# Keeping the keys and values of the last twelve batches on chip for a second cross attention, and exchanging two copies

## What is computed

```python
q = heads(LN(x) @ Wq.T + bq)        # 16 heads of 16 features
k = heads(ctx @ Wk.T + bk)          # ctx: 64 batches x 257 rows x 256
v = heads(ctx @ Wv.T + bv)
attn = softmax(q @ k.T / 4)         # per batch and head: 32 x 257
x = x + merge(attn @ v) @ Wo.T + bo
```

## Time and profile before

| what | value |
|---|---|
| device time, median of 3 runs | 1705.42 us (1704.83 to 1706.88) |
| the profiled execution | 1704.21 us, of which the span is 1702.4 us |
| busy in the span | PE 91%, PE weight loads 71%, DVE 68%, ACT 48%, POOL 35% |
| DMA | 218.43 MB, mean 128 GB/s |
| mean granted TensorE clock | 0.955 of full speed |

### The profile page before, as it was taken

How to read it: one execution, slowest core, us unless ns; L and a number is a source line. 1 busy time by engine, 2 the same in 40 slices (tenths; PEclk the granted TensorE clock), 3 DMA queues, 4 the chain that set the end, 5 groups by cost and what they waited for, 6 DMA issues and landing times. The chain is left out here.

```text
span 1702.4 us, 39132 instructions
## 1 busy us (share of the span) xinstructions
PE 1550.2 (91%) x15530; PEld 1204.2 (71%) x15530; DVE 1153.1 (68%) x2441; ACT 813.4 (48%) x1815; POOL 594.9 (35%) x501
## 2 busy tenths in 40 slices
PE   6988989999998899999999788888889788999998
PEld 3444467555576589999998555666678688599997
DVE  4576869982057456777762446888689777578887
ACT  1232752121134436666664327777637622566664
POOL 2330200000011047865633325677559653112210
PEclk8897999999989989999999899999989899999999
DMA  9993049621023467676745854766200010001001
GB/s 293 325 318 98 1 145 226 125 54 44 1 93 112 121 197 271 241 242 205 235 152 145 244 184 136 230 201 197 80 25 1 16 29 4 13 13 38 20 7 50
DMA packets 151364, 218.43 MB, mean 128 GB/s; under 512 B 38353, under 2 KB 124753, under 8 KB 145297
## 3 DMA queue, kind: packets, MB, share of 16 engines
q1 hardware_dynamic: 115008, 107.80, 22.6%
q0 software_dynamic: 10368, 58.47, 10.7%
q10 hardware_dynamic: 25808, 49.68, 9.0%
HBM read 168.85 MB, written 47.05 MB: 127 GB/s over the span
## 5 line engine op out<-in xcount | busy, mean ns | idle before, releaser
L321 PE MATMUL ps<-kv_ctx,kv_w 128*128 128x257 f32 x512 | 138.6, 407 | 18.9 <-PEq L1743 8.1
L2209 POOL TENSOR_TENSOR a_pr<-a_pr,a_inv 128x1028 f32<-128x1028 f32 x64 | 121.9, 1906 | 71.8 <-DVE a_inv L2321 71.4
L325 PE MATMUL ps<-kv_w,kv_ctx 128*128 128x256 f32 x512 | 131.6, 403 | 13.7 <-ACT kv_kv L345 13.7
L321 PEld LDWEIGHTS ps<-kv_ctx,kv_w 128*128 128x128 f32 x512 | 97.7, 203 | 41.1 <-issue 16.4
L325 PEld LDWEIGHTS ps<-kv_w,kv_ctx 128*128 128x128 f32 x512 | 99.8, 201 | 37.1 <-ACT kv_kv L345 22.0
L2297 ACT ACTIVATE a_pr<-ps,a_neg 128x257 f32<-128x257 f32 x256 | 117.8, 480 | 0.6 <-DVE a_neg L2340 0.6
L1556 POOL TENSOR_TENSOR b0m_pm<-b_dr,b_gates 128x256 f32<-128x256 f32 x16 | 13.2, 831 | 289.7 <-SPq L1520 260.8
L111 PE MATMUL ps<-f_xTH,f_w1H 128*128 128x256 f32 x368 | 106.7, 290 | 1.5 <-DVE f_xTL L1952 1.5
L2046 DVE TENSOR_TENSOR f_hL<-f_hr,f_hH 128x512 fp32r<-128x512 f32 x92 | 75.6, 847 | 45.3 <-ACT f_hH L1895 45.2
L3190 DVE SCALAR_TENSOR_TENSOR x<-ps,g_gate,x 128x256 f32<-128x256 f32 x256 | 105.2, 475 | 0.0
L112 PE MATMUL ps<-f_xTL,f_w1H 128*128 128x256 f32 x368 | 104.8, 285 | 0.0
(11 more groups left out here) (416 smaller groups left out, 4470.5 us busy)
## 6 DMA issues: line engine op xcount, KB each, us to landing
a_kv<-kv SPq DMA_DIRECT2D x64, 513.0 KB, 4.0
kv<-kv_kv ACTq DMA_DIRECT2D x53, 513.0 KB, 5.7
a_ctxT<-in_ctxT SPq DMA_DIRECT2D x32, 514.0 KB, 8.0
a_ctxR<-in_ctx SPq DMA_DIRECT2D x32, 512.0 KB
kv_ctx<-in_ctxT ACTq DMA_DIRECT2D x61, 257.0 KB, 3.3
outs<-f_yo SPq DMA_DIRECT2D x23, 256.0 KB, 2.6
a_vB<-vlast SPq DMA_DIRECT2D x16, 256.0 KB
kv<-f_kv ACTq DMA_DIRECT2D x5, 513.0 KB, 10.6
```

The source lines that it names most:

```text
L321: done = e.matmul(out[:, 0:NK], self.w[:, 0, c, cols(part)], ctx[:, c, :], start=(c == 0), stop=(c == DC - 1))
L325: done = e.matmul(out[:, cols(t, D)], ctx[:, c, cols(t)], self.w[:, 1, c, :], start=(c == 0), stop=(c == DC - 1))
L2209: e.tensor_tensor(pr[:, b % RP, :, :], pr[:, b % RP, :, :], inv[:, b % 2, :].unsqueeze(2).to_broadcast([P, HG, NK]), ALU.mult).then_inc(*p ...
```

## The change

The last twelve batches (52 to 63) are no longer stored and loaded again. Their keys and values are written straight into a tile of twelve places (KeysKept) where the loop reads them; it lies where the expert layer held its first weights and one half of its hidden values. Batches 52 to 56 are formed there in the expert layer's tail, 57 to 63 in the second cross attention. The loop takes these twelve first: its i-th batch is (i + 52) mod 64, and the later ones are loaded twelve ahead into the same places. The values of the last key are stored in the new order, in two pieces, and loaded four batches at a time. The row tiles of x are finished in the new order. In the loop VectorE now copies the first turn and ScalarE the second, one step later; ScalarE also does the first instruction of the weighted pair; the exponents and the maxima are split in two halves with other work between them. The weighting of a new pair waits for the pair before it, where it waited for the one two before.

```diff
@@ -31,6 +31,7 @@
+KEPT = 12
@@ -263,6 +265,33 @@
+class KeysKept:
...
+    def __init__(self, K):
+        self.Y = Layer(K, "late")
+        self.at = self.Y.sb("kv", [P, KEPT, KV])
...
+    def places(self, first, last):
+        return [KeptPlace(self.at[:, b - (B - KEPT), :]) for b in range(first, last)]
...
+    def close(self):
+        self.Y.close()
...
+class KeptPlace:
...
+    def __init__(self, at):
+        self.at = at
...
+    def free(self, e):
+        pass
...
+    def store(self, e, out):
+        pass
@@ -1666,6 +1695,10 @@
+    with Layer(K, "f0w") as Y:
+        w1 = [Y.sb(f"w1{n}", [P, 2, DC, FC * P], F32R) for n in "HL"]
+        high = Y.sb("hH", [P, 2, FC, BLOCK], F32R)
+    K.late = KeysKept(K)
@@ -1733,8 +1765,9 @@
-        A.host(AHEAD[4], (0, 1, 2, 3), A.own + [kv2, kv3, kv1])
-        assert AHEAD[4] % 5 == 2
+        first, kept = sum(AHEAD[:4]), B - KEPT
+        stored = [(A.own + [kv2, kv3, kv1])[n % 5] for n in range(kept - first)]
+        A.host(AHEAD[4], (0, 1, 2, 3), stored + K.late.places(kept, first + AHEAD[4]))
@@ -2064,7 +2097,7 @@
-    HG, RV, LB, SB, RP, RAMP = 4, 8, 8, 6, 4, 4
+    HG, RV, LB, SB, RP, RAMP = 4, KEPT, 4, 6, 4, 4
@@ -2072,21 +2105,23 @@
-        kv = sb("kv", [P, RV, KV])
+        kv = K.late.at
...
         neg, tot, inv = (sb(n, [P, 2, HG]) for n in ("neg", "tot", "inv"))
...
-        def load(e, b):
-            e.dma_start(kv[:, b % RV, :], K.kv[b]).then_inc(*ld_kv[b % RV].up(16))
+        def batch(i):
+            return (i + B - KEPT) % B
...
+        def load(e, i):
+            e.dma_start(kv[:, i % RV, :], K.kv[batch(i)]).then_inc(*ld_kv[i % RV].up(16))
@@ -2100,7 +2135,7 @@
-            A.host(AHEAD[5], (6, 7), A.own + [kv1])
+            A.host(AHEAD[5], (6, 7), K.late.places(B - AHEAD[5], B))
@@ -2124,11 +2159,10 @@
-                    for b in range(RV):
-                        load(e, b)
...
-                    e.dma_start(K.vlast, vlm[:, :]).then_inc(*d_vl.up(16))
-                    e.wait_ge(*d_vl.at(16))
+                    e.dma_start(K.vlast[0:KEPT, :], vlm[B - KEPT:B, :]).then_inc(*d_vl.up(16))
+                    e.dma_start(K.vlast[KEPT:B, :], vlm[0:B - KEPT, :]).then_inc(*d_vl.up(16))
+                    e.wait_ge(*d_vl.at(32))
                     for j in range(2):
@@ -2172,13 +2206,16 @@
+        rows = [batch(BT * n) // BT for n in range(NT)]
+        K.norms["s"].order = rows
@@ -2208,28 +2245,31 @@
-                    if b >= 2 * LB and b % 2:
-                        K.next.piece(e, (b - 2 * LB) // 2)
+                    if b >= 16 and b % 2:
+                        K.next.piece(e, (b - 16) // 2)
...
                 def scores(b):
-                    e.wait_ge(*ld_kv[b % RV].at(16 * (b // RV + 1)))
+                    if b < KEPT:
+                        e.wait_ge(*A.ev.at(3 * (batch(b) + 1)))
+                    else:
+                        e.wait_ge(*ld_kv[b % RV].at(16 * (b // RV)))
                     if b:
...
-                                            qb[own, c, b, :, :].rearrange("p h q -> p (h q)"), kT(b, c)[own, :], start=True, stop=True)
+                                            qb[own, c, batch(b), :, :].rearrange("p h q -> p (h q)"), kT(b, c)[own, :], start=True, stop=True)
...
                     if t:
-                        e.wait_ge(*a_T.at(b + 1))
+                        e.wait_ge(*v_T.at(b + 1))
                     elif b:
-                        e.wait_ge(*v_T.at(b))
+                        e.wait_ge(*a_T.at(b))
                     for r in range(HG):
@@ -2237,8 +2277,8 @@
-                    if b >= 4:
-                        e.wait_ge(*v_oT.at((b - 4) // 2 + 1))
+                    if b >= 2:
+                        e.wait_ge(*v_oT.at((b - 2) // 2 + 1))
@@ -2285,31 +2325,43 @@
             def _(e):
-                def exponents(b):
-                    if b >= 2:
-                        e.wait_ge(*v_inv.at(b - 1))
-                    if b >= RP:
-                        e.wait_ge(*t_T.at(2 * (b - RP) + 2))
-                        e.wait_ge(*v_last.at(b - RP + 1))
-                    for r in range(HG):
-                        if r % 2 == 0:
-                            e.wait_ge(*v_mx.at(2 * b + r // 2 + 1))
+                def exponents(b, side):
+                    if side == 0:
+                        if b >= 2:
+                            e.wait_ge(*v_inv.at(b - 1))
+                        if b >= RP:
+                            e.wait_ge(*t_T.at(2 * (b - RP) + 2))
+                            e.wait_ge(*v_last.at(b - RP + 1))
+                    e.wait_ge(*v_mx.at(2 * b + side + 1))
+                    for r in (2 * side, 2 * side + 1):
...
                 def turned(b):
-                    e.wait_ge(*t_T.at(2 * b + 1))
+                    e.wait_ge(*t_T.at(2 * b + 2))
                     if b >= 2:
...
-                    e.activation(prT[:, b % 2, 0, :, :], K.ps[:, 6, :].rearrange("p (g n) -> p g n", g=HG), ACT.Copy).then_inc(*a_T.up())
-                for i in range(B + 4):
+                    e.activation(prT[:, b % 2, 1, :, :], K.ps[:, 6, :].rearrange("p (g n) -> p g n", g=HG), ACT.Copy).then_inc(*a_T.up())
...
+                def half_weighed(n):
...
+                    e.wait_ge(*t_P.at(2 * n + 2))
+                    if n:
+                        e.wait_ge(*v_oT.at(n))
+                    out = out_pair(n).rearrange("p c b (h q) -> p c b h q", h=2)
+                    e.activation(half[:, :, :, :], out[:, :, :, 0, :], ACT.Copy, scale=K.parity[:, 0:1]).then_inc(*a_half.up())
...
+                for i in range(B + 5):
                     if has(i - 1):
-                        exponents(i - 1)
+                        exponents(i - 1, 0)
+                    if i % 2 == 0 and has(i - 6):
+                        half_weighed((i - 6) // 2)
+                    if has(i - 4):
+                        turned(i - 4)
+                    if has(i - 1):
+                        exponents(i - 1, 1)
                     if i < 3:
...
-                    if has(i - 3):
-                        turned(i - 3)
@@ -2322,45 +2374,45 @@
-                    e.wait_ge(*t_P.at(2 * n + 2))
-                    if n:
-                        e.wait_ge(*v_oT.at(n))
+                    e.wait_ge(*a_half.at(n + 1))
...
-                    e.tensor_scalar(half[:, :, :, :], out[:, :, :, 0, :], K.parity[:, 0:1], None, ALU.mult).then_inc(*v_half.up())
-                    e.wait_ge(*v_half.at(n + 1))
-                    e.scalar_tensor_tensor(oT[:, :, cols(n, 2 * L)].rearrange("p c (b q) -> p c b q", b=2), out[:, :, :, 1, :],
+                    at = batch(2 * n) // 2
+                    e.scalar_tensor_tensor(oT[:, :, cols(at, 2 * L)].rearrange("p c (b q) -> p c b q", b=2), out[:, :, :, 1, :],
...
-                def maxima(b):
+                def maxima(b, side):
...
-                    for r in (0, 2):
-                        at = bank(b, r)
-                        e.tensor_reduce(neg[:, b % 2, r:r + 2], K.ps[:, at:at + 2, 0:NK], AX.X, ALU.max, negate=True).then_inc(*v_mx.up())
+                    r = 2 * side
+                    at = bank(b, r)
+                    e.tensor_reduce(neg[:, b % 2, r:r + 2], K.ps[:, at:at + 2, 0:NK], AX.X, ALU.max, negate=True).then_inc(*v_mx.up())
...
                 def turned(b):
-                    e.wait_ge(*t_T.at(2 * b + 2))
+                    e.wait_ge(*t_T.at(2 * b + 1))
                     if b >= 2:
...
-                    e.tensor_copy(prT[:, b % 2, 1, :, :], K.ps[:, 6, :].rearrange("p (g n) -> p g n", g=HG)).then_inc(*v_T.up())
+                    e.tensor_copy(prT[:, b % 2, 0, :, :], K.ps[:, 6, :].rearrange("p (g n) -> p g n", g=HG)).then_inc(*v_T.up())
...
-                for i in range(B + 4):
...
+                for i in range(B + 5):
+                    if i % 2 == 0 and has(i - 6):
+                        weighed((i - 6) // 2)
                     if has(i):
-                        maxima(i)
+                        maxima(i, 0)
+                    if has(i - 3):
+                        turned(i - 3)
+                    if has(i):
+                        maxima(i, 1)
                     if has(i - 1):
...
-                    if has(i - 4) and i % 2:
-                        weighed((i - 4) // 2)
-                    if has(i - 3):
-                        turned(i - 3)
                 for t in range(NT):
@@ -2369,20 +2421,21 @@
             def _(e):
-                for b in range(RV, B):
-                    e.wait_ge(*t_P.at(b - RV + 1))
-                    load(e, b)
-                    done = b - RV + 1
+                for done in range(1, B - LB):
+                    e.wait_ge(*t_P.at(done))
+                    if done - 1 + RV < B:
+                        load(e, done - 1 + RV)
...
-                    if done % LB == 0 and 2 <= j < B // LB:
+                    if done % LB == 0 and j < B // LB:
...
-                    if done == LB:
```

(4 more changed lines are left out.)

34 lines of the change are left out of this document (17 added, 17 removed).

## The result

The changed kernel took 1676.65 us (median of 4 runs, 1675.34 to 1688.1), the kernel before 1705.12 on the same chip: a ratio of 0.9848, 95% interval 0.9804 to 0.9893. It is 28.5 us faster by the medians. The forecast was 1689.5 with a range from 1682 to 1698, so the sign was right and the forecast gain of 15.6 us was too small by almost half. Medians and ratios in this document leave out the few executions that ran in a slower state of the chip.

What follows compares the result with a forecast made beforehand. A ring of waits, no engine full, was taken to set the loop's pace, crowded DMA the stretches ahead. Terms 1.8 + 5.4 + 0.3 + 8.1 = 15.6 us off the median 1705.42 gave 1689.8, said as 1689.5; range 1682 to 1698.

Steps and rivals of the forecast that it cites:

- Batch loop and its drain: Second cross attention's batch loop and tail: exchanged copies bring 3.025 us a batch to 2.89, 8.1 us over 60.
- Steps of the ring: Batch loop: two transpose sets sharing a PSUM bank and their copies, steps 0.67, 0.74, 0.66, 0.82, sum 2.89 us.
- the single stumbles: Batch loop: 2.7 us above 57 x 3.025 in the kernel before, left in by the forecast.
- Rival 2: Batch loop goes under the ring's floor, exponents' path decides at 2.75 us a batch: 1681; chance 0.12.
- Query stage: Before the batch loop: dropped stores, loads and buffer waits give back 5.4 us, from 3 to 6.
- Tail: End of the first expert layer: last gather sooner without five stores, and no last store; 1.8 us, 0.3 to 2.9.
- First batches: Start of the batch loop: ScalarE's store just ahead of its exponential table load goes, 0.3 us.
- Rival 4: Kept keys' layout costs something elsewhere, or the transfers' relief is swallowed: within 3 us of before, 1703; chance 0.04.
- Rival 1: Batch loop: the exchange does nothing, another queue takes its place, only the transfers pay: 1698; chance 0.14.
- rival 3: Batch loop: last values, loaded four batches at a time, come late and VectorE waits: slower, up to 1756; chance 0.04.

Runs made afterwards that it cites:

- the first pair: Profiles of the kernel before and the changed kernel shown with the result: 1705.12 and 1676.65 us, ratio 0.9848.
- the lengthened ring: Changed kernel plus a one-column ScalarE copy in each batch, between the wait for the second transposes and their copy: 1690.41 us (0.9860).
- the first experiments' chip: Chip of four kernels against the kernel before: kept keys only 0.9908, exchange only 0.9971, kernel before again 0.9999, changed kernel again 0.9886.
- the exchange alone: Kernel before, all keys stored and loaded, plus swapped copies, split maxima and exponents, and ScalarE's mask: 0.9971 (0.9948 to 0.9993).
- the third pair: Kernel before and changed kernel, both unchanged, run again on a later chip: 1699.49 and 1674.90 us, ratio 0.9842.
- the experiment with stores: Changed kernel, but the twelve kept batches are also stored, 513 KB each, and still not loaded: 1693.89 us, 0.9886.
- the kernel with the places alone: Kernel before with only the SBUF tile places of the change, nothing kept and nothing exchanged: 0.9977 (0.9950 to 1.0003).
- the two halves: Each half of the change alone against the kernel before: kept keys only 0.9908, exchanged copies with split maxima, exponents and ScalarE mask 0.9971.

## Why the prediction was too small

The mechanisms named were all there. The miss is in the size of the tail, and in what had no term: the places of tiles, TensorE's clock ahead of the loop, and the difference between two executions. In the first pair, against which the forecast stands, most of the miss is what had no term: 8.98 + 1.77 of the 28.5 us lie outside the stretches that were priced, and these came to 16.95 against 15.6. That they came so near is luck: there the tail's larger gain was hidden.

- **Batch loop and its drain, forecast 8.1.** Right: 8.51 in the first pair, 8.48 in the third. Steps of the ring, period and equal batches came as written. That the sum fits to 0.4 us is in part luck: the period fell by 0.115 and not 0.135, which is 6.6 us over 57 batches, and the other 1.8 came from the single stumbles, which the forecast left in at 2.7 us and of which 0.9 remained. Rival 2, a ring under its floor, is out: the period is 2.91, not 2.75, and the lengthened ring answers with 0.09.
- **Query stage, forecast 5.4, from 3 to 6.** 4.98 in the first pair; over the profiles 49.0 us in five with the old stores and buffers and 42.4 in the seven of kept keys without added stores or loads, 6.6. But two things are mixed in this. One is the time that TensorE lost in waits, which the forecast priced: TensorE's idle time fell from between 5.4 and 8.5 us to 2.0 in each of the seven. The other is its clock, which had no term: the seven differ among themselves by 2.9 us (40.6 to 43.5) at the same idle time, with granted clocks from 1.00 to 0.93. The cleanest comparison is of two kernels of the first experiments' chip, both at 1.00, the exchange alone and then the changed kernel (window, length, then busy time of TensorE, its weight loads, VectorE, ScalarE and GpSimd; clock, DMA share, GB/s):

```profile
985.43:1030.75 45.32, 39.90 (x161) 26.77 (x161) 19.60 (x34) 13.11 (x33) 10.99 (x16) 1.00 0.81 238
981.69:1022.31 40.62, 38.63 (x160) 26.74 (x161) 19.59 (x34) 13.67 (x33) 10.98 (x16) 1.00 0.26 72
```

  That is 4.7 us, within the range and near the 5.4. The stores by themselves are 1.0 of it (idle time 3.0 against 2.0 us with and without them) and the loads by themselves nothing. By elimination the other 3.7 are ScalarE's waits for buffers, or stores and loads acting together; these two were not separated.
- **Tail, forecast 1.8, from 0.3 to 2.9.** This is the step that failed, and by its reason. It let the last gather start 1.1 us sooner and gave it the lowest landing of the earlier trace rows, 5.7 us. The last gathers did not start sooner. They landed in 2.7, since the stores that shared the 16 DMA engines with them at the end were gone. The lowest landing under load is no floor for a landing without load. The sum also had a slip: a landing counts from the start of the issue (the last gather after starts at 950.40 and its addition 2.74 later), and the forecast added the 5.7 to the end of the issue, 956.9 instead of 956.0, which made the term 0.9 us too small by its own numbers. The page of the Trainium skill that the prediction weighed (DMA: Bandwidth & Descriptors, Anatomy of one DMA) gave an estimated 2.3 us for a gather without traffic, and 3.4 us more in the sum; the trace after agrees with it to 0.4 us. The first pair showed only 2.33 in the tail, inside the range by luck, because its gathers took 2.28 longer to start (46.77 us from first to last, against 44.49), which ate half of the 4.20 us won behind the last one (6.94 against 2.74); the third pair shows the 5.95, and the experiment with stores 7.2.
- **First batches, forecast 0.3.** 1.13 and 3.96 in the two pairs, 25.1 against 23.3 us over the profiles. Here too the length goes with TensorE's clock, 0.74 to 0.93 in the profiles. The two kernels of the third pair stood at 0.74 and 0.92, those of the first pair at 0.80 and 0.79, and at 0.93 and 0.92 the kernel with the places alone took 22.90 and the changed one 22.17. So at the same clock the change gives 0.7 to 1.1 us, and the rest is the clock. The forecast had counted the shorter period from the seventh batch on only; six batches of 0.115 are another 0.7. Whether the change itself raises the clock is not shown.
- **No term: the places of tiles.** 1.8 us in the expert layer ahead of the tail over all profiles, 2.3 in the first pair. Rival 4 had thought of a cost of the layout; it was a gain.

Together 1.8 (places) + 5.9 (tail, by the third pair) + 6.6 (query stage) + 1.8 (first batches) + 8.5 (loop) = 24.6 us, of which 2 to 3 are the clock's. It lies between the 19.5 us of the chip whose tail hides its share and the 26.8 of the third pair. The first pair's 28.5 contain besides what two executions differ by: of the 8.98 us ahead of the first gather, 6.71 lie ahead of the expert layer (its last table load stands at 626.76 and 620.05), in code that is the same on every engine, and the changed kernel's own profiles differ by 6.1 us there (618.62 and 624.72, on two chips).

Rival 1 (the exchange does nothing) fell by the two halves, rival 3 (last values late) by VectorE's waits from the seventh S to the last, where its only large one is for the scores, 26.1 us in all; rival 4 by the ratio.

## What to carry to other kernels

Where a stretch ends with transfers, the last ones land without company once the other traffic is gone: price them by a landing with idle DMA engines beside it, not by the shortest one under load. A loop bound by a ring of waits is sized by adding up the measured steps, start to start, and each instruction in it counts by how much it delays the next start. Cut two profiles at the same events before explaining a difference, and read the part that is the same program first: here it held a quarter of it. Where one engine is nearly full in a stretch, compare its idle time and its granted clock apart, since the length mixes the two.

## What the runs showed of the hardware

- The same matmul of 256 columns takes 283 ns or 281 by where its tiles lie in SBUF, 0.7%, alike in every profile; the one matmul whose tiles got no new place of this kind did not gain (283, 284).
- A gather of 128 KB took 5.7 to 9.9 us to land with the DMA engines 0.9 busy, and 2.7 with them 0.34 busy.
- The query stage took 40.6 us at a clock of 1.00 and 43.5 at 0.93, with 2.0 us of idle TensorE in both.
- On one chip of four the handing over between TensorE and ScalarE crept for some 30 us in the tail, with waits of 7 to 12 us of ScalarE that have no recorded releaser, in all four kernels profiled there.
- An activation of one column lasts 0.20 us and delays the next by 0.11, as the lengthened ring shows it.
